# A graph kernel: 16 step registers for a block in place of 32, and the PSUM slot worked out from the edge tile

## The reference

```
edge_index = stack([src, dst])
h = relu(layernorm(x));  x = x + L0(h, edge_index)                # graph diffusion
h = relu(layernorm(x));  x = x + L1(h, edge_weight, edge_type)    # one of 8 weights for an edge, messages summed by dst
h = relu(layernorm(x));  x = x + L2(h, edge_index, edge_attr)     # two attention convolutions, then a skip layer
h = relu(layernorm(x));  x = x + L3(h, edge_index)                # two GCN convolutions (widths 32 and 64)

out = segment_sum(msg, dst, num_segments=n)                       # the sum that each of them ends with
```

## Time and profile before

| | |
|---|---|
| three runs, median (lowest to highest) | 8047.32 us (8043.76 to 8050.65) |
| profiled execution: device time | 8050.76 us |
| its span, first to last instruction | 8048.9 us |
| granted TensorE clock, mean | 0.802 |
| TensorE busy | 62% |
| VectorE busy | 57% |
| GpSimd busy | 52% |

### The profile page before, as it was taken

One profiled execution on the slowest core, in us unless ns is written; L12 is line 12 of the kernel. 1 busy time (PEld: TensorE's weight loads), 2 busy tenths in 40 slices (PEclk: granted clock), 3 DMA queues, 4 the chain that ended last, 5 costly groups with the idle time before them and its releaser, 6 DMA issues. The chain is left out here.

```text
span 8048.9 us, 102237 instructions
## 1 busy us (share of the span) xinstructions
PE 4999.5 (62%) x32610; PEld 4427.0 (55%) x32610; DVE 4617.5 (57%) x5704; ACT 1145.0 (14%) x1724; POOL 4173.2 (52%) x3346
## 2 busy tenths in 40 slices
PE   4555334664078876555556866666587774674687
PEld 2344234554077765555555756666576763563565
DVE  6999543112577765666667642222475983672347
ACT  0133111221043200222220001111000430000001
POOL 0288566654077400777770037777300007877886
PEclk9855666777589999666668987777799987897899
DMA  1276565545922355223323543434365872112009
GB/s 69 73 212 211 149 134 119 102 94 127 332 71 72 91 189 171 75 77 80 80 77 114 192 148 111 111 111 111 90 193 191 310 283 68 46 52 79 11 11 256
DMA packets 836386, 1024.65 MB, mean 127 GB/s; under 512 B 587119, under 2 KB 600324, under 8 KB 834892
## 3 DMA queue, kind: packets, MB, share of 16 engines
q1 hardware_dynamic: 501260, 626.23, 25.6%
q10 hardware_dynamic: 190528, 303.71, 10.6%
q0 software_dynamic: 144256, 90.12, 7.7%
HBM read 608.19 MB, written 417.84 MB: 127 GB/s over the span
## 5 line engine op out<-in xcount | busy, mean ns | idle before, releaser
L830 POOL DMA_INDIRECT gc_msgs<-t,src_rows x784 | 963.4, 1229 | 1153.8 <-POOLq L145 888.4
L880 POOL DMA_INDIRECT acc<-de_sums,de_put x392 | 682.0, 1740 | 450.3 <-DMA acc<-de_sums,de_put 175.1
L1867 PE MATMUL gc_ps<-gc_msgs,gc_hot 128*128 x4736 | 659.0, 306 | 365.6 <-SPq L1831 365.6
L1867 PEld LDWEIGHTS gc_ps<-gc_msgs,gc_hot 128*128 128x128 f32 x4736 | 639.2, 220 | 417.8 <-issue 415.6
L830 POOL DMA_INDIRECT at1s_ends<-x,src_rows x392 | 395.9, 1010 | 580.1 <-POOLq L145 461.0
L830 POOL DMA_INDIRECT at2s_ends<-h,src_rows x392 | 370.3, 945 | 617.6 <-POOLq L145 498.5
L830 POOL DMA_INDIRECT at1s_ends<-x,dst_rows x392 | 419.1, 1069 | 119.4 <-issue 119.4
L830 POOL DMA_INDIRECT re_rows<-x,src_rows x392 | 406.1, 1036 | 133.8 <-issue 124.2
L1009 PE MATMUL de_ps<-de_win,de_pick 128*128 x2368 | 420.8, 351 | 77.8 <-ACT de_pick L1025 41.7
L1009 PEld LDWEIGHTS de_ps<-de_win,de_pick 128*128 128x128 f32 x2368 | 404.9, 262 | 107.9 <-issue 101.1
L992 PE MATMUL de_ps_pick<-de_near,de_hot 128*128 x1184 | 152.5, 272 | 482.4 <-issue 427.6
(11 more groups left out here) (450 smaller groups left out, 11928.0 us busy)
## 6 DMA issues: line engine op xcount, KB each, us to landing
rew_win<-x SPq DMA_DIRECT2D x74, 544.0 KB, 5.1
at1w_win<-g SPq DMA_DIRECT2D x74, 544.0 KB, 4.9
at2w_win<-g SPq DMA_DIRECT2D x74, 544.0 KB, 4.9
de_win<-t SPq DMA_DIRECT2D x74, 512.0 KB, 4.4
de_near<-same SPq DMA_DIRECT2D x74, 512.0 KB, 5.5
x<-rew_win ACTq DMA_DIRECT2D x74, 512.0 KB, 5.0
h<-at1w_win ACTq DMA_DIRECT2D x74, 512.0 KB, 4.9
h<-at2w_win ACTq DMA_DIRECT2D x74, 512.0 KB, 5.1
```

Of the source, the lines that this page charges most:

```text
L830: nc.gpsimd.indirect_dma_start(buf[:, t * width:(t + 1) * width], None, table, bass.IndirectOffsetOnAxis(ap=rows[:, t:t + 1], axis=0)).the ...
L880: nc.gpsimd.indirect_dma_start(g.acc0[j % 2], bass.IndirectOffsetOnAxis(ap=put[:, j:j + 1], axis=0), sums[:, j * D:(j + 1) * D], None, com ...
L1867: done = nc.tensor.matmul(ps[k][:, bass.ds(to[n], SLOT)], hot[k][:, n, :], each_group(msgs[:, bass.ds(of[n], MID)], SLOT // MID), start=Fa ...
```

## The change

The load of line 1146 takes 16 registers in place of 32, the edge tiles alone. The slot of a step is computed by PE's sequencer: (edge tile of the block's first step + n - edge tile of step n) times the slot's width. That is `at`, since each step moves on by one tile of either kind. In the attention merges the register holds the edge tile times 64, so both terms are multiplied by 2. In "rew" it holds the bare edge tile, whose offset in the messages is then also computed (times 65), and the table's fifth part is a copy in place of a product.

```
-                v.tensor_scalar(g.steps[:, 4 * S:5 * S], edge[:, :], float(D + 1), None, ALU.mult)
+                v.tensor_copy(g.steps[:, 4 * S:5 * S], edge[:, :])
```

```
-                    regs = [nc.tensor.alloc_register(f"{name}_step{m}_{n}") for n in range(2 * S)]
-                    first = S if counts is None else 3 * S
-                    wide = D if counts is None else D + 1
-                    nc.tensor.load(regs, g.steps[m:m + 1, first:first + 2 * S])
-                    slot = [pe.snap(x, donate=True, min_val=0, max_val=(S - 1) * SLOT) for x in regs[0:S]]
-                    of = [pe.snap(x, donate=True, min_val=0, max_val=(T - 1) * wide) for x in regs[S:2 * S]]
+                    regs = [nc.tensor.alloc_register(f"{name}_step{m}_{n}") for n in range(S)]
+                    first, unit = (2 * S, D) if counts is None else (4 * S, 1)
+                    nc.tensor.load(regs, g.steps[m:m + 1, first:first + S])
+                    at = [pe.snap(x, donate=True, min_val=0, max_val=(T - 1) * unit) for x in regs]
+                    of = at if counts is None else [x * (D + 1) for x in at]
+                    slot = [nc.s_assert_within((at[0] * (SLOT // unit) + n * SLOT) - at[n] * (SLOT // unit), 0, (S - 1) * SLOT,
+                                               skip_runtime_bounds_check_because="a step moves on by one tile of edges or of nodes") for n in range(S)]
```

## The result

| | before | after |
|---|---|---|
| runs beside each other, median (lowest to highest) | 8045.54 us (8039.13 to 8050.65) | 8204.75 us (8200.23 to 8217.89) |
| span of the profiled execution | 8048.9 us | 8203.0 us |
| granted TensorE clock, mean | 0.802 | 0.806 |
| TensorE, VectorE, GpSimd busy | 62%, 57%, 52% | 64%, 56%, 51% |

The ratio is 1.0201, with a 95% interval of 1.0183 to 1.0219: the change makes the kernel 2.0% slower, some 159 us. The forecast was 8013, the range ended at 8150. What came is the third rival: the register work costs more than the shorter load gives.

What follows compares the result with a forecast made beforehand. PE's sequencer was taken to bound the merges at 5.70 us a block; a shorter load less dearer register work gave 5.55, 33 us over 221 blocks plus 1, hence 8013 us, range 7955 to 8150.

Steps and rivals of the forecast that it cites:

- third rival: In the merges, register work above 0.259 us a step outweighs the shorter load; at 0.30, 97 us slower, 8144; chance 0.20.
- What bounds the kernel: In the three merges PE's sequencer, not the array, sets the pace: 5.70 us a block, the array needing 4.4.
- 0.33 a step: Slower case with a third register instruction per step: the burst is over before the load, block 6.50 us, time 8220.
- Term 1: PE's register load per block: 16 in place of 32 take off 1.02 us, leaving 1.10, plus slowing by the DMA burst.
- my formula: Block time C: load's start plus 0.065 + 1.10 + 0.5 x (6.38 - C), the last bracket being the load's burst cover.
- the 0.5: Slowing of the register load, in us for each us of full DMA burst, with 0.25 and 0.7 as ends.
- Term 2: PE's register work per step: 0.245 us against 0.133, in two instructions, moving the load's start from 2.47 to 3.97 us.
- The two together: In a merge block the later, shorter load meets another part of the DMA burst: 5.55 us, a gain of 0.15.
- slower rival: The third rival: register work costs more than the shorter load gives, 8144 or, with a third instruction, 8220; chance 0.20.
- The next limit: DVE comes next after PE's sequencer, able to do a block of "rew" in some 4.6 to 4.9 us.
- second rival: One instruction takes all of a step's register work, 0.165 us; block 5.05 us, 144 us faster, 7903; chance 0.12.

Runs made afterwards that it cites:

- e2: The changed kernel, arithmetic kept, loading 32 registers again, 16 of them unused: 9684.78 against 9308.44 us for the kernel before, ratio 1.0425.
- e5: The changed kernel with addresses in bytes, so a step's six operations fit one instruction: ratio 0.9989 to the kernel before, 0.9964 when run again.
- h3: The kernel before, loading 16 registers (first edge tile, fifteen slots) and computing the message tile, subtraction first of six operations: 9285.08 against 9310.43 us, ratio 0.9964.
- g1: The kernel before, 32 registers loaded, with one addition of two registers more per step, third of five operations: 8056.83 against 8050.07 us, ratio 1.0013.
- e3: The kernel before, attention merges loading only 16 slots, used for both addresses without added arithmetic (sums not the reference's): 9302.21 us, ratio 0.9996.
- f3: e3 with a quarter of each store, and each merge first copying its whole source to the destination: 8024.91 against 8051.6 us, ratio 0.9967.

## Why the prediction was wrong

*What bounds the kernel: right.* e2 lengthens the load alone and every block follows by the same 1.03 us. The datapaths had room throughout. Two small slips: "at1w" of the kernel before stands at 5.66, not between 5.69 and 5.73 (the mean of the three is 5.70 all the same), and for 0.33 a step the sum is 8224, not 8220.

*Term 1: right in the quiet; the burst stood elsewhere.* The load of 16 is 1.13 us behind the burst (forecast 1.10). The 64 ns a register hold: 32 take 2.18 in e2. The Trainium skill's 200 ns for a register ("Runtime: NRT & Kernel Launch", Instruction fetch mechanics) would make these loads 3.2 and 6.4, an estimate; the traces do not agree. But e5, whose load starts at 3.75, should by my formula have blocks of (3.75 + 1.165 + 3.19) / 1.5 = 5.40, and has 5.57 to 5.65. The formula lets the burst cover 6.38 - 5.40 = 1.0 us of that load. In e5 it covers all 1.74 and goes on for some 0.4 behind it, because the store waits for the landing before and leaves 0.7 to 0.95 us after its sum. So a part of e5's excess is the store chain, which I had left out, and e5 does not price the 0.5 by itself. For a load wholly in the burst the runs give 0.4 us a us (e5: 0.6 more in 1.74) to 0.6 (h3: 1.7 more in 2.8).

*Term 2: this step failed.* Its structure held: six operations fit one instruction, the seventh opens a second, the pause was 59 ns (0.06), the second instruction 42 or 32 (35), 78 to the next. The first instruction was 143 ns, not 73. I had priced every operation at 9 ns from rows in which all are on one register and a constant; a subtraction of two registers, behind other operations, was not among them. The 151 ns of line 1864 stood in my own rows as the warning. 0.322 a step in place of 0.245, 16 times, moves the load's start from 3.97 to 5.20 to 5.35. The rule of the Trainium skill ("Perfetto Trace Analysis", Per-engine timelines, Sequencer-only Instruction), that the profile shows only part of what such an instruction takes, holds here: 137 ns of a step's 322 lie between the records, 59 between two register instructions in a row and 78 up to the next step, with the product in between in the program.

*The two together: right in kind.* With the start at 5.20, past the end of the burst, the sum is 5.20 + 0.065 + 1.10 = 6.37 us, and "at1w" has 6.38. That is the case that I had worked out for 0.33 a step (6.50, 8220, measured 8204.75), but I had put it down to a third instruction, so that its number came close for another reason, and gave the whole slower rival 0.20, though 0.014 us a step lay between it and the forecast. The range should have held the 8220 that I had computed. g1 shows the same exchange: what is added ahead of a load inside the burst is free as far as it moves the load out of it.

*The next limit: wrong.* I named DVE, at 4.6 to 4.9. It is the window traffic, at about 5.5 (e3, h3, f3). It left my 5.55 just possible, but the second rival's 5.05 and 7903 could not have come: h3 is one cheap instruction a step, and gains 25 us, not 144. And e5, with a step of 0.221, less than the 0.245 I had forecast, gained 18 to 28 us; so even if a step had cost what I forecast, the 33 would have been somewhat too much.

Not settled: why a two-register operation is dear behind others in an instruction, and whether it is its place there or the address that it belongs to; and what a block would be if only the order of the stores were loosened, with all bytes kept.

## What to carry to other kernels

Fewer registers to load are worth 64 ns each, once a block, if the load stands in a quiet stretch; in a burst of DMA the load of 16 took up to 2.8 us here in the median, hardly less than the 3.1 of 32. Each operation that replaces them is paid at every step, so count sixteen steps against one load, and look at whether the work still fits one instruction and whether a two-register operation comes first in it. Before forecasting a gain on a sequencer, find what the next bound is by taking the work away, not by reading the idle time of an engine: here a store chain stood 0.2 us behind a sequencer that looked like the only limit. It could be seen beforehand, in how many stores leave just after the landing before (21 of 46 in "at2w"). When your own rows hold one figure that your price does not explain, the price is not known yet.

## What the runs showed of the hardware

- One instruction of register operations on TensorE's sequencer: 46 ns with three operations (e3), 55 with four, 74 with six, all on constants. With a two-register operation first: 53 (four, addition), 60 (four, subtraction), 63 (five, addition), 79 (six, subtraction). With it third or later: 120 (five, addition), 126 (five, subtraction), 138 to 143 (six). Numbers of operations and their places are counted in the program.
- A seventh operation opens a second instruction: 59 ns of pause and its own 32 to 42.
- A load of 16 registers takes 1.13 us with the DMA engines quiet, and in a burst 1.74 (e5) to 2.8 (h3, and "at1w" of e3), by where in the burst it starts; one of 32 takes 2.18 and 3.1.
- A 512 KB store beside a 544 KB window load takes 5.3 us from issue to landing (e3) and a 128 KB one 3.6 (f3). The next store of the chain leaves 0.2 us after the landing.
